# Edge tiles of a graph kernel: a 16-bit view of the source one-hots in place of a copy, and the fourth source one-hot made on ScalarE

## The chip, the cores and the metric

The kernel runs on one NeuronCore of a Trainium2 chip as a single launch. The metric is the device time of one execution in microseconds (us); lower is better. The engines are named as in the profile: PE (TensorE matmuls), PEld (TensorE weight loads), DVE (VectorE), ACT (ScalarE), POOL (GpSimd) and SP (the queue that issues most transfers). A "q" behind an engine's name marks its sequencer, which handles registers, waits and DMA issues.

## What is computed

Four graph layers follow one another on 3,125 nodes of 128 features and 103,125 edges. The stage of this case is the edge pass of the first layer, and what later layers need of the edges is gathered in the same pass:

```python
edge_index = jnp.stack([src, dst])
h = jnp.maximum(_layernorm(x), 0.0)
# layer 0: one message per edge, summed at the edge's source
msg_input = jnp.concatenate([h[dst], edge_feats], axis=1)
m = leaky_relu(msg_input @ msg_w1 + msg_b1)
messages = m @ msg_w2 + msg_b2
aggregated = segment_sum(messages, src, num_segments=3125)
# layers 1 to 3 sum over the same edges at dst: plain, or weighted by rel_table[etype]
```

## The kernel before, in words

An earlier stage sorts the edges by (source tile, destination tile). The edge stage then takes them in tiles of 128 edges, four tiles (`G` = 4) to a group. There are 1,504 tiles, so 376 groups, handled as 47 passes of `RING` = 8 groups (`LOOPS` = 47). The first pass and the last are written out; on VectorE the 45 passes between run as one hardware loop with a body of eight steps, in which semaphore counts come from registers.

For each group the stage builds one-hot matrices that place edges at nodes, and multiplies with them:

- `ohd` (16 bit): destination one-hots, four tiles in one VectorE instruction (function `onehots` on VectorE).
- `ohs` (32 bit): source one-hots. GpSimd makes the first three tiles (`onehots` on GpSimd, semaphore `s_os`), VectorE the fourth (`source_onehot`, semaphore `s_o3`).
- `ohs16`: a 16-bit copy of `ohs`, made by ScalarE in one instruction (line 1014). In the profile buffer numbers are dropped, so it is printed as `ohs_e` too.
- `ohw`: `ohd` scaled by each edge's relation weight, four ScalarE instructions (line 1016).
- TensorE turns `ohd` (`pdt`, line 1041), ScalarE copies that to `dT` (line 1007), and TensorE multiplies `dT` with node projections into `px`, three matmuls a tile (line 1070).
- VectorE adds the rows of the edges to `px`, which gives `pre` (function `add`, line 1125). ScalarE makes the negative part (`excess`, line 1000), GpSimd adds both to `hid` (line 973), and TensorE sums `hid` over the sources into `ps` (line 1081). VectorE adds `ps` to `S` (line 1151).
- The pair products `pm` are two matmuls a tile: `ohs16` by `ohd` (line 1063) and `ohs` by `ohw` (line 1064). `pm` has two halves, tiles 0 and 1 of a group in the one, tiles 2 and 3 in the other. VectorE adds each tile's `pm` to a running sum `acc` (function `collect`, line 1137), one after the other, since each sum starts from the one before.

No planner sets the order; each engine's `step` writes it by hand. A VectorE step is: collect tile 0, `source_onehot` of the next group, collect tile 1, `add`, a table lookup into a register (`place`, lines 62 and 1130), collect tile 2, `onehots`, collect tile 3, `sums`. In TensorE's `tiles`, the first matmul of tile 2 waits until the collects have freed the second half of `pm`, that is until tile 3 of the group before has been collected:

```python
if j % 2 == 0 and not (first and kp < 1):
    pe.wait_ge(s_acc, (m - 1) * G + 2 * q + 2)
```

The last `px` matmul of the step raises `s_x`, for which `add` waits.

Of the kernel before, what the change touches and what calls it, by code (L numbers as in the profile page):

```python
# [15 lines left out]
BF16 = mybir.dt.bfloat16  # L16
I32 = mybir.dt.int32
ALU = mybir.AluOpType
ACT = mybir.ActivationFunctionType
# [3 lines left out]
P = 128  # L23
D = 128
# [14 lines left out]
G = 4  # L39
RING = 8  # L40
BUFS = 4
# [13 lines left out]
def back(i, k, n):  # L55

    return (i + (k - n) // RING if (k - n) // RING else i), (k - n) % RING
# [21 lines left out]
def build(nc, x, src, dst, ea, et, w1, b1, w2, b2, u1, c1, u2, c2,  # L79
# [6 lines left out]
    with ExitStack() as top:  # L86
# [3 lines left out]
        def sem(name):  # L90
            return top.enter_context(nc.semaphore(name))
# [5 lines left out]
        iota128 = tsb("iota128", [P, P])  # L97
# [5 lines left out]
        ones = tsb("ones", [P, P])  # L103
# [31 lines left out]
        with ExitStack() as srt:  # L135
            def sb(name, shape, dt=F32):
                return srt.enter_context(nc.sbuf_tensor(name, shape, dt))
# [727 lines left out]
        with ExitStack() as ctx:  # L865
# [9 lines left out]
            ohd = sb("ohd_e", [P, BUFS, G, P], BF16)  # L875
            ohw = sb("ohw_e", [P, BUFS, G, P])
            ohs = sb("ohs_e", [P, BUFS, G, P])
            ohs16 = sb("ohs16_e", [P, BUFS, G, P], BF16)
            dT = sb("dT", [P, 2, G, P], BF16)
            pre = sb("pre_e", [P, 2, G, P])  # L880
            excess = sb("excess", [P, 2, G, P])
# [9 lines left out]
            s_od = sem("e_dst_onehots")  # L891
            s_os = sem("e_src_onehots")
            s_o3 = sem("e_last_src_onehot")
            s_o16 = sem("e_src_onehots16")
            s_td = sem("e_dst_turned")
            s_cd = sem("e_dst_copied")
            s_x = sem("e_hidden")
# [56 lines left out]
            @block.gpsimd  # L954
            def _(pool):
                def onehots(i, k, first):
                    n = i * RING + k
                    pool.wait_ge(s_rt[k // 2], i * 16 + 16)
                    if not (first and k < BUFS):
                        pool.wait_ge(s_sp, n - BUFS + 1)  # L960
                        pool.wait_ge(s_o16, n - BUFS + 1)
                    pool.sem_inc(s_go, 1)
                    for j in range(G - 1):
                        last = nc.gpsimd.tensor_scalar(ohs[:, k % BUFS, j, :], iota128[:], rt[:, k, j, D + 1:D + 2], None, ALU.is_equal)  # L964
                    last.then_inc(s_os, 1)

                def leaky(i, k, first):
                    n = i * RING + k
                    pool.wait_ge(s_y, n + 1)
                    if not (first and k < 2):  # L970
                        pool.wait_ge(s_sp, n - 1)
                    pool.sem_inc(s_go, 1)
                    nc.gpsimd.tensor_tensor(hid[:, k % 2, :, 0:D], pre[:, k % 2, :, :], excess[:, k % 2, :, :],  # L973
                                            ALU.add).then_inc(s_g, 1)

                onehots(0, 0, True)
                for k in range(RING):
                    onehots(*back(0, k, -1), k + 1 < RING)
                    if k:
                        leaky(0, k - 1, True)  # L980
                    else:
                        nc.gpsimd.memset(S[:], 0.0).then_inc(s_sz, 1)
                with pool.Fori(1, LOOPS - 1) as i:
                    for k in range(RING):
                        onehots(*back(i, k, -1), False)
                        leaky(*back(i, k, 1), False)
                for k in range(RING):
                    if k + 1 < RING:
                        onehots(LOOPS - 1, k + 1, False)
                    leaky(*back(LOOPS - 1, k, 1), False)  # L990
                leaky(LOOPS - 1, RING - 1, False)

            @block.scalar
            def _(act):
                def negative(i, k, first):
                    n = i * RING + k
                    act.wait_ge(s_pre, n + 1)
                    if not (first and k < 2):
                        act.wait_ge(s_g, n - 1)
                    nc.scalar.activation(excess[:, k % 2, :, :], pre[:, k % 2, :, :], ACT.Relu, scale=-0.8).then_inc(s_y, 1)  # L1000

                def step(i, k, first, final):
                    n = i * RING + k
                    if not (first and k < 2):
                        act.wait_ge(s_x, n - 1)
                    act.wait_ge(s_td, n + 1)
                    nc.scalar.activation(dT[:, k % 2, :, :], pdt[:, k % 2, 0:G, :], ACT.Copy).then_inc(s_cd, 1)  # L1007
                    if not (first and k < 1):
                        negative(*back(i, k, 1), first)
                    if not (first and k < BUFS):  # L1010
                        act.wait_ge(s_m, 2 * (n - BUFS) + 2)
                    act.wait_ge(s_os, n + 1)
                    act.wait_ge(s_o3, n + 1)
                    nc.scalar.activation(ohs16[:, k % BUFS, :, :], ohs[:, k % BUFS, :, :], ACT.Copy).then_inc(s_o16, 1)  # L1014
                    for j in range(G):
                        last = nc.scalar.activation(ohw[:, k % BUFS, j, :], ohd[:, k % BUFS, j, :], ACT.Copy, scale=rt[:, k, j, D + 2:D + 3])  # L1016
                    last.then_inc(s_ow, 1)
                    if not (first and k == 0):
                        load_freed(act, i, k, final)

                for k in range(RING):
                    step(0, k, True, False)
                with act.Fori(1, LOOPS - 1) as i:
                    for k in range(RING):
                        step(i, k, False, False)
                for k in range(RING):
                    step(LOOPS - 1, k, False, True)
                negative(LOOPS - 1, RING - 1, False)

            @block.tensor  # L1030
            def _(pe):
# [12 lines left out]
                def tiles(hid_of, pair_of, first):  # L1044
# [9 lines left out]
                    if pair_of:  # L1054
                        ip, kp = pair_of
                        m = ip * RING + kp
                        pe.wait_ge(s_ow, m + 1)
                    for j in range(G):
                        if pair_of:
                            q = j // 2  # L1060
# [43 lines left out]
            def _(dve):  # L1104
# [45 lines left out]
                    Sv = S[:, ds(st, 1), :].squeeze(1)  # L1150
                    nc.vector.tensor_tensor(Sv, Sv, ps[:, k % 2, 0:D + 1], ALU.add).then_inc(s_sa, 1)

                def source_onehot(i, k, first):

                    n = i * RING + k
                    dve.wait_ge(s_rt[k // 2], i * 16 + 16)
                    if not (first and k < BUFS):
                        dve.wait_ge(s_sp, n - BUFS + 1)
                    nc.vector.tensor_scalar(ohs[:, k % BUFS, G - 1, :], iota128[:], rt[:, k, G - 1, D + 1:D + 2], None,
                                            ALU.is_equal).then_inc(s_o3, 1)  # L1160

                def step(i, k, first, final):

                    one, two, three = (not (first and k < n) for n in (1, 2, 3))
                    if two:
                        collect(*back(i, k, 2), first, 0)
                    if not (final and k == RING - 1):
                        source_onehot(*back(i, k, -1), first and k + 1 < RING)
                    if two:
                        collect(*back(i, k, 2), first, 1)  # L1170
                    if one:
# [13 lines left out]

                onehots(0, 0, True)
                onehots(0, 1, True)
                source_onehot(0, 0, True)
                for k in range(RING):
                    step(0, k, True, False)  # L1190
                with dve.Fori(1, LOOPS - 1) as i:
# [1026 lines left out]
```

## Time and profile before

| what | value |
|---|---|
| time of a run, median of 3 | 3433.16 us |
| lowest and highest of the 3 | 3431.87 and 3433.22 us |
| profiled execution, span from first to last instruction | 3432.5 us |
| first and last `collect` of the edge stage | 1330.4 and 2637.1 us from the span's start |
| granted TensorE clock through the edge stage | 1.00 of full speed |

The span is the profiled execution's own time; it lies 0.7 us under the median of the runs. Times in the rows further down count from the span's start. A row of a timeline gives start, duration, engine, line and operation, what is written and read, how many instructions are merged, and in brackets how long the engine had been idle and who ended that. Idle times of some tens of nanoseconds are not printed.

### The profile page before, as it was taken

What the parts mean: (1) busy time and instruction counts of PE and PEld (TensorE: products, weight loads), DVE (VectorE), ACT (ScalarE), POOL (GpSimd) and SP (SyncE); (2) the same over time, 40 slices, a digit from 0 to 9 for tenths busy, and PEclk for the clock granted to TensorE, in tenths of its full rate; (3) what the DMA queues carried; (4) which work ended last, traced back from release to release, by engine and by line L of the source; (5) the groups of instructions that cost most, each with busy time, mean ns of one, the idle gap of its engine ahead of it and who ended that gap; (6) DMA issues with size and microseconds to landing.
All of it is one profiled execution on the core that took longest, in us unless ns stands there. A gap on an engine that the chain in (4) does not pass through costs nothing. (4 is left out here: it accounts for less than half of the span.)

```text
span 3432.5 us, 87712 instructions
## 1 busy us (share of the span) xinstructions
PE 2529.2 (74%) x20390; PEld 1959.9 (57%) x20391; DVE 2686.0 (78%) x8325; ACT 1648.7 (48%) x4130; POOL 1979.1 (58%) x2344
## 2 busy tenths in 40 slices
PE   2433555555555555999999999999999329989899
PEld 1322334443334434888888888888887214444454
DVE  8853777777777765999999999999997779993501
ACT  2011222222222224888888888888886655452200
POOL 1005777777777777888888888888887000000000
PEclk9976666677666677999999999999999559999999
DMA  9993222222222215888888888888887569868766
GB/s 382 412 414 117 79 78 78 78 78 83 78 77 78 78 63 145 230 227 229 230 227 228 231 225 228 231 227 230 228 227 244 215 284 352 300 235 304 250 218 203
DMA packets 738172, 696.85 MB, mean 203 GB/s; under 512 B 48523, under 2 KB 637274, under 8 KB 734778
## 3 DMA queue, kind: packets, MB, share of 16 engines
q1 hardware_dynamic: 516770, 536.77, 46.7%
q10 hardware_dynamic: 195544, 104.71, 12.6%
q0 software_dynamic: 25792, 54.52, 4.8%
q8 instruction: 37, 0.61, 0.1%
q14 instruction: 29, 0.24, 0.0%
HBM read 340.91 MB, written 354.90 MB: 203 GB/s over the span
## 5 line engine op out<-in xcount | busy, mean ns | idle before, releaser
L855 POOL DMA_INDIRECT sorted_rows<-rows,posi x806 | 784.1, 973 | 338.9 <-issue 316.6
L1137 DVE SCALAR_TENSOR_TENSOR acc<-acc,keep,pm 128x256 f32<-128x256 f32 x1504 | 717.4, 477 | 23.0 <-issue 8.3
L964 POOL TENSOR_SCALAR ohs_e<-iota,rt 128x128 f32<-128x128 f32 x1128 | 663.6, 603 | 12.5 <-DMA rt<-sorted_rows 12.5
L1064 PE MATMUL pm<-ohw_e,ohs_e 128*128 128x128 f32 x3008 | 662.6, 302 | 0.0
L803 PE MATMUL s_peq<-sb_w1bb,eT 128*128 128x256 f32 x806 | 352.2, 531 | 397.7 <-ACT eT L658 378.8
L973 POOL TENSOR_TENSOR hid<-pre_e,excess 128x512 f32<-128x512 f32 x376 | 511.8, 1361 | 141.6 <-ACT excess L1000 141.6
L1070 PE MATMUL px<-PN,dT 128*128 x4512 | 498.3, 219 | 0.1
L1016 ACT ACTIVATE ohw_e<-ohd_e,rt 128x128 f32<-128x128 bf16 x1504 | 474.6, 386 | 0.0
L1064 PEld LDWEIGHTS pm<-ohw_e,ohs_e 128*128 128x128 f32 x3008 | 459.4, 193 | 0.0
L803 PEld LDWEIGHTS s_peq<-sb_w1bb,eT 128*128 128x128 f32 x806 | 172.6, 264 | 439.4 <-ACT eT L658 431.1
L1081 PE MATMUL ps<-hid,ohs_e 128*128 128x129 f32 x3008 | 417.9, 281 | 1.2 <-POOL hid L973 1.1
L1070 PEld LDWEIGHTS px<-PN,dT 128*128 128x128 bf16 x4512 | 382.4, 99 | 18.2 <-issue 0.3
L1063 PE MATMUL pm<-ohd_e,ohs_e 128*128 128x128 bf16 x1504 | 334.0, 222 | 48.2 <-DVE acc L1137 11.8
L1081 PEld LDWEIGHTS ps<-hid,ohs_e 128*128 128x128 f32 x3008 | 365.5, 191 | 1.7 <-POOL hid L973 1.5
L1000 ACT ACTIVATE excess<-pre_e 128x512 f32<-128x512 f32 x376 | 237.3, 631 | 255.2 <-DVE pre_e L1125 255.2
L721 DVE SCALAR_TENSOR_TENSOR junkR<-s_binrows,binc,later 128x128 bf16<-128x128 f32 x806 | 235.1, 346 | 77.8 <-PE s_binrows L776 77.8
L651 ACT ACTIVATE rows<-lo 128x26 f32 (+1 forms) x62 | 15.4, 249 | 543.9 <-DMA sorted_rows<-rows,posi 468.7
L1125 DVE TENSOR_TENSOR pre_e<-px,rt 128x512 f32<-128x512 f32 x376 | 258.6, 688 | 14.6 <-PE px L1070 3.4
L1117 DVE TENSOR_TENSOR ohd_e<-iota,rt 128x512 bf16<-128x512 bf16 x376 | 257.1, 684 | 0.2 <-DVEq L1109 0.2
L1007 ACT ACTIVATE dT<-pdt 128x512 bf16<-128x512 bf16 x376 | 216.0, 575 | 40.3 <-PE pdt L1041 40.3
L1014 ACT ACTIVATE ohs_e<-ohs_e 128x512 bf16<-128x512 f32 x376 | 230.5, 613 | 0.0
L701 DVE SCALAR_TENSOR_TENSOR junkW<-iotar,typc,relt 128x100 bf16<-128x100 f32 x806 | 224.7, 321 | 2.2
(317 smaller groups left out, 4275.0 us busy)
## 6 DMA issues: line engine op xcount, KB each, us to landing
count_matrices<-acc SPq DMA_DIRECT2D x1504, 128.0 KB, 2.4
sorted_rows<-zrow SPq DMA_DIRECT2D x188, 528.0 KB, 10.1
rt<-sorted_rows ACTq DMA_DIRECT2D x184, 528.0 KB, 4.5
gab<-count_matrices SPq DMA_DIRECT2D x60, 1280.0 KB, 6.0
arb<-count_matrices SPq DMA_DIRECT2D x25, 1664.0 KB, 9.0
ab<-count_matrices SPq DMA_DIRECT2D x25, 1600.0 KB, 9.0
arb<-count_matrices SPq DMA_DIRECT2D x25, 1536.0 KB, 8.4
ef<-in_edge_attr_dram SPq DMA_DIRECT2D x58, 364.0 KB
```

What stands on the lines that cost most here:

```text
L803: nc.tensor.matmul(pe_q[:, q % 2, 0:2 * D], eT[:, q % 2, :], w1bb[:], start=True, stop=True).then_inc(s_q, 1)
L855: pool.indirect_dma_start(sortd, bass.IndirectOffsetOnAxis(ap=posi[:, h, c:c + 1], axis=0), rows[:, h, c, :], None).then_inc(s_sc[h], 16)
L964: last = nc.gpsimd.tensor_scalar(ohs[:, k % BUFS, j, :], iota128[:], rt[:, k, j, D + 1:D + 2], None, ALU.is_equal)
L973: nc.gpsimd.tensor_tensor(hid[:, k % 2, :, 0:D], pre[:, k % 2, :, :], excess[:, k % 2, :, :], ALU.add).then_inc(s_g, 1)
L1016: last = nc.scalar.activation(ohw[:, k % BUFS, j, :], ohd[:, k % BUFS, j, :], ACT.Copy, scale=rt[:, k, j, D + 2:D + 3])
L1063: nc.tensor.matmul(pm[:, q, j % 2, 0:P], ohs16[:, kp % BUFS, j, :], ohd[:, kp % BUFS, j, :], start=True, stop=True)
L1064: last = nc.tensor.matmul(pm[:, q, j % 2, P:2 * P], ohs[:, kp % BUFS, j, :], ohw[:, kp % BUFS, j, :], start=True, stop=True)
L1070: last = nc.tensor.matmul(px[:, kh % 2, j, :], dT[:, kh % 2, j, :], PN[:, ds(dt[j], 1), part, :].squeeze(1), start=(part == 0), stop=(part ...
L1081: last = nc.tensor.matmul(ps[:, k % 2, 0:D + 1], ohs[:, k % BUFS, j, :], hid[:, k % 2, j, :], start=(j == 0), stop=(j == G - 1))
L1117: nc.vector.tensor_tensor(ohd[:, k % BUFS, :, :], iota16[:].unsqueeze(1).to_broadcast([P, G, P]), rt[:, k, :, D:D + 1].to_broadcast([P, G, ...
L1125: nc.vector.tensor_tensor(pre[:, k % 2, :, :], px[:, k % 2, :, :], rt[:, k, :, 0:D], ALU.add).then_inc(s_pre, 1)
L1137: nc.vector.scalar_tensor_tensor(acc[:, k % SUMS, j, :], before, keep[:, at:at + 1] if isinstance(at, int) else keep[:, ds(at, 1)], pm[:, ...
```

## The change

The 16-bit copy `ohs16` goes: the name becomes a view of `ohs` that takes the upper 16 bits of each 32-bit value, so the matmul at line 1063 loads its weights with a step of two 16-bit elements. The upper half of the 32-bit numbers 0 and 1 are the 16-bit numbers 0 and 1. The fourth source one-hot moves from VectorE to ScalarE as two instructions: `distances` takes the absolute value of (column minus source) into a new tile `far`, and `nearest` takes Relu(1 - `far`). TensorE now waits for the source one-hots itself, and GpSimd no longer waits for the copy.

```diff
-            ohs16 = sb("ohs16_e", [P, BUFS, G, P], BF16)
+            ohs16 = ohs[:].bitcast(BF16).rearrange("p b j (c h) -> p b j c h", h=2)[:, :, :, :, 1]
+            far = sb("far_e", [P, 2, P])
...
-            s_o16 = sem("e_src_onehots16")
+            s_far = sem("e_last_src_distances")
...
-                        pool.wait_ge(s_o16, n - BUFS + 1)
...
+                def distances(i, k, first):
+                    n = i * RING + k
+                    act.wait_ge(s_rt[k // 2], i * 16 + 16)
+                    if not (first and k < 2):
+                        act.wait_ge(s_o3, n - 1)
+                    nc.scalar.activation(far[:, k % 2, :], iota128[:], ACT.Abs, bias=rt[:, k, G - 1, D + 1:D + 2],
+                                         scale=-1.0).then_inc(s_far, 1)
+
+                def nearest(i, k, first):
+                    n = i * RING + k
+                    act.wait_ge(s_far, n + 1)
+                    if not (first and k < BUFS):
+                        act.wait_ge(s_sp, n - BUFS + 1)
+                    nc.scalar.activation(ohs[:, k % BUFS, G - 1, :], far[:, k % 2, :], ACT.Relu, bias=ones[:, 0:1],
+                                         scale=-1.0).then_inc(s_o3, 1)
...
+                    distances(i, k, first)
...
-                    act.wait_ge(s_os, n + 1)
-                    act.wait_ge(s_o3, n + 1)
-                    nc.scalar.activation(ohs16[:, k % BUFS, :, :], ohs[:, k % BUFS, :, :], ACT.Copy).then_inc(s_o16, 1)
...
+                    nearest(i, k, first)
...
+                        pe.wait_ge(s_os, m + 1)
+                        pe.wait_ge(s_o3, m + 1)
...
-                def source_onehot(i, k, first):
...
-                    if not (final and k == RING - 1):
-                        source_onehot(*back(i, k, -1), first and k + 1 < RING)
```

In the built program, an `ISA` or `REGISTER_ALU` row is a sequencer instruction on registers; a wait in brackets stands on that row and holds up what follows. On VectorE, in the second step of the loop's body, these rows stood from the collect of tile 0 to `pre`:

```order
L1137 SCALAR_TENSOR_TENSOR acc<-acc,keep,pm 128x256
L1158 REGISTER_ALU [waits e_rows1]
L1159 TENSOR_SCALAR ohs_e<-iota,rt 128x128 [waits e_group_sums]
L1134 REGISTER_ALU
L1137 ISA [waits e_accumulated]
L1137 SCALAR_TENSOR_TENSOR acc<-acc,keep,pm 128x256
L1122 REGISTER_ALU
L1125 TENSOR_TENSOR pre_e<-px,rt 128x512 [waits e_leaky,e_hidden]
```

In the changed kernel the same place reads:

```order
L1154 SCALAR_TENSOR_TENSOR acc<-acc,keep,pm 128x256
L1151 REGISTER_ALU
L1154 ISA [waits e_accumulated]
L1154 SCALAR_TENSOR_TENSOR acc<-acc,keep,pm 128x256
L1139 REGISTER_ALU
L1141 REGISTER_ALU [waits e_hidden]
L1142 TENSOR_TENSOR pre_e<-px,rt 128x512 [waits e_leaky]
```

The one-hot is gone, the collect of tile 1 still waits for that of tile 0 (`e_accumulated`) on the register row ahead of it, and the wait for `px` (`e_hidden`) has moved from `pre` itself to a register row ahead of `pre`. In the body's other seven steps it stays on `pre`.

On TensorE, at the start of the loop's body, these rows lead to the first pair product before:

```order
L62 TENSOR_LOAD tilei
L1051 REGISTER_ALU
L1053 REGISTER_ALU [waits e_dst_copied]
L1062 ISA [waits e_weighted_onehots,e_pre]
L1063 MATMUL pm<-ohd_e,ohs_e 128x128 [waits e_accumulated]
```

And in the changed kernel:

```order
L62 TENSOR_LOAD tilei
L1066 REGISTER_ALU
L1068 REGISTER_ALU [waits e_dst_copied]
L1079 ISA [waits e_src_onehots,e_last_src_onehot,e_weighted_onehots,e_pre]
L1080 MATMUL pm<-ohd_e,ohs_e 128x128 [waits e_accumulated]
```

Two waits are added there, as in every step; the matmuls and their order stay.

On ScalarE, the rows of a step of the body from the copy or the weighted one-hots to `dT` were:

```order
L1014 ACTIVATE ohs_e<-ohs_e 128x512 [waits e_last_src_onehot,e_src_onehots,e_pair_products]
L1016 ACTIVATE ohw_e<-ohd_e,rt 128x128 x4
L1006 REGISTER_ALU [waits e_hidden]
L1007 ACTIVATE dT<-pdt 128x512 [waits e_dst_turned]
L1000 ACTIVATE excess<-pre_e 128x512 [waits e_leaky,e_pre]
```

They are now:

```order
L1030 ACTIVATE ohw_e<-ohd_e,rt 128x128 [waits e_pair_products]
L1030 ACTIVATE ohw_e<-ohd_e,rt 128x128 x3
L1014 REGISTER_ALU [waits e_last_src_distances]
L1015 ACTIVATE ohs_e<-far_e,ones 128x128 [waits e_group_sums]
L1007 ACTIVATE far_e<-iota,rt 128x128 [waits e_last_src_onehot,e_rows1]
L1023 REGISTER_ALU [waits e_hidden]
L1024 ACTIVATE dT<-pdt 128x512 [waits e_dst_turned]
```

One instruction of 512 columns ahead of the weighted one-hots is replaced by two of 128 columns behind them. No table load stands among the body's ScalarE rows in either kernel.

## Rows read from the trace of the kernel before

**Rows 1.** The page's first line.

```profile
span 3432.5 us, 87712 instructions
```

**Rows 2.** Stretches: busy us and instructions per engine, PE clock, DMA share, GB/s.

```profile
2000.00:2100.00 100.00, 96.40 (x1039) 89.89 (x1040) 97.66 (x231) 80.50 (x202) 89.32 (x116) 1.00 0.84 229
```

**Rows 3.** Timeline of VectorE, one step of the loop (start, duration in us).

```profile
2000.12 0.48 DVE L1137 SCALAR_TENSOR_TENSOR acc<-acc,keep,pm 128x256 f32<-128x256 f32 x1
2000.52 0.29 DVE L1159 TENSOR_SCALAR ohs_e<-iota,rt 128x128 f32<-128x128 f32 x1
2000.74 0.48 DVE L1137 SCALAR_TENSOR_TENSOR acc<-acc,keep,pm 128x256 f32<-128x256 f32 x1
2001.26 0.69 DVE L1125 TENSOR_TENSOR pre_e<-px,rt 128x512 f32<-128x512 f32 x1
2001.98 0.48 DVE L1137 SCALAR_TENSOR_TENSOR acc<-acc,keep,pm 128x256 f32<-128x256 f32 x1
...
2002.98 0.47 DVE L1137 SCALAR_TENSOR_TENSOR acc<-acc,keep,pm 128x256 f32<-128x256 f32 x1
...
2004.72 0.69 DVE L1125 TENSOR_TENSOR pre_e<-px,rt 128x512 f32<-128x512 f32 x1
```

**Rows 4.** Timeline of TensorE's matmuls, same stretch.

```profile
2000.89 0.33 PE L1070 MATMUL px<-PN,dT 128*128 x3
...
2003.51 0.23 PE L1063 MATMUL pm<-ohd_e,ohs_e 128*128 128x128 bf16 x1
...
2004.36 0.33 PE L1070 MATMUL px<-PN,dT 128*128 x3
2004.52 1.11 PE L1081 MATMUL ps<-hid,ohs_e 128*128 128x129 f32 x8
2005.47 0.39 PE L1041 MATMUL pdt<-ident,ohd_e 128*128 128x128 bf16 x4
```

**Rows 5.** Waits from 1600 to 2500 us: total us, times, longest us.

```profile
ACT excess L1000 <- DVE pre_e L1125: 175.7, 259, 1.0
...
PEld pm L1063 <- DVE acc L1137: 76.9, 255, 0.4
```

**Rows 6.** Sequencer instructions of two lines: count, ns min/median/max, first and last start.

```profile
L62 DVEq TENSOR_LOAD <-tilei x259: 303/308/440, 1601.3 to 2498.6; - x130
...
L1057 PEldq EVENT_SEMAPHORE  x259: 51/51/51, 1602.2 to 2498.9; - x130
```

**Rows 7.** Timeline of VectorE, first two steps of a loop pass.

```profile
2021.18 0.48 DVE L1137 SCALAR_TENSOR_TENSOR acc<-acc,keep,pm 128x256 f32<-128x256 f32 x1 [0.20 <-issue]
...
2021.87 0.47 DVE L1137 SCALAR_TENSOR_TENSOR acc<-acc,keep,pm 128x256 f32<-128x256 f32 x1
2022.26 0.68 DVE L1125 TENSOR_TENSOR pre_e<-px,rt 128x512 f32<-128x512 f32 x1
2022.86 0.46 DVE L1137 SCALAR_TENSOR_TENSOR acc<-acc,keep,pm 128x256 f32<-128x256 f32 x1
...
2025.61 0.68 DVE L1125 TENSOR_TENSOR pre_e<-px,rt 128x512 f32<-128x512 f32 x1
2026.31 0.48 DVE L1137 SCALAR_TENSOR_TENSOR acc<-acc,keep,pm 128x256 f32<-128x256 f32 x1
```

**Rows 8.** Timeline of TensorE's matmuls, same two steps.

```profile
2019.83 0.23 PE L1063 MATMUL pm<-ohd_e,ohs_e 128*128 128x128 bf16 x1
...
2020.84 0.23 PE L1063 MATMUL pm<-ohd_e,ohs_e 128*128 128x128 bf16 x1
...
2021.69 0.33 PE L1070 MATMUL px<-PN,dT 128*128 x3
...
2025.22 0.33 PE L1070 MATMUL px<-PN,dT 128*128 x3
```

**Rows 9.** Timeline of ScalarE: the copy and the four weighted one-hots.

```profile
2002.52 0.61 ACT L1014 ACTIVATE ohs_e<-ohs_e 128x512 bf16<-128x512 f32 x1
...
2003.04 1.26 ACT L1016 ACTIVATE ohw_e<-ohd_e,rt 128x128 f32<-128x128 bf16 x4
```

More of the change, by code:

```diff
@@ L1151, in sums @@
                     nc.vector.tensor_tensor(Sv, Sv, ps[:, k % 2, 0:D + 1], ALU.add).then_inc(s_sa, 1)
-                def source_onehot(i, k, first):
[L1155 to L1160, printed above, removed]
                 def step(i, k, first, final):
@@ L1187, in _ @@
                 onehots(0, 1, True)
-                source_onehot(0, 0, True)
                 for k in range(RING):
```

## The prediction

> **What bounds the kernel now.** I read the stretches first. Every 100 us of the edge stage look like [rows 2]: VectorE busy 97.7, TensorE 96.4, GpSimd 89, ScalarE 80.5, all at full TensorE clock. That invites the reading "VectorE is the bound, so taking an instruction from it pays". Two engines at 96 and 98% do not say which one the other waits for, so I went to the timelines of one step, looking for gaps between an end and the next start.
>
> The step takes 3.46 us (`pre` at 2001.26 and at 2004.72, [rows 3]). Follow it from the collect of tile 3. That ends at 2002.98 + 0.47 = 2003.45, and TensorE starts tile 2's pair product at 2003.51 [rows 3, 4]. It had been idle: the waits say that weight loads of `pm` waited for `acc` in 255 of 259 steps, 76.9 us in all, 0.30 us each [rows 5]. TensorE then does the second half of its tiles, whose last `px` ends at 2004.36 + 0.33 = 2004.69, and VectorE starts `pre` at 2004.72, 0.03 later [rows 3, 4]. One step earlier it is the same: `px` ends at 2001.22, `pre` starts at 2001.26. Yet the collect before it started at 2000.74, and two VectorE instructions that do not wait for each other start some 0.40 apart here (collect of tile 0 to the one-hot, 2000.12 to 2000.52); `pre` could have gone at 2001.14. So `pre` waits for TensorE, only too briefly to be printed. From `pre` it is 0.72 to the collect of tile 2 and 1.00 from there to that of tile 3, which closes the ring:
>
> 0.47 + 0.06 + 1.18 + 0.03 + 0.72 + 1.00 = 3.46 us.
>
> That is the whole step. The 0.72 is more than the 0.60 that `pre` needs before the next instruction may start (2022.26 to 2022.86, [rows 7], where VectorE was late). The difference is the sequencer: held at `pre` by the wait, it only then begins the table lookup, 0.31 us for the load alone [rows 6], and the register work for the next collect.
>
> The removed one-hot is not in this ring. It stands between the collects of tiles 0 and 1, and these depend on each other: the first ends at 2000.60, the second starts at 2000.74, 0.13 to 0.14 later, with the one-hot done in between [rows 3]. The wait between them stands on a register row, and 0.13 is what that costs: 0.04 as at `pre`, where the wait is on the instruction itself, and some 0.09 for the register row.
>
> **The change part by part.**
>
> - *One-hot off VectorE.* 0.29 busy, 0.22 of start to start (2000.52 to 2000.74). In an ordinary step it filled a gap that the collects need anyway, and `pre` waits for TensorE behind it: worth 0. The gap stays, now empty.
> - *Copy off ScalarE, two short instructions on.* The copy held ScalarE for 0.52 (2002.52 to 3.04); the one-hots on 128 columns take 1.26 for four, so at most 0.32 each [rows 9]. I take the new two at that price, since they have the same width and one operand per partition like them: 0.64 − 0.52 = +0.12 a step. ScalarE idles 175.7 / 259 = 0.68 us a step waiting for `pre` [rows 5], so 0. Below, nothing excludes their being as short as nothing; above, the 0.61 of the copy each would be +0.70, just more than the cover, but that row has four times the columns. Queued behind them are the load of rows several steps ahead and `dT`; `dT` moves by the same +0.12, which would lie under the 0.30 for which TensorE waits later in its step. GpSimd's dropped wait was not one that ended last: 0.
> - *Weights with a step of two.* No row shows such a load. Nearest are the contiguous 16-bit ones, with `px` matmuls 0.16 / 3 = 0.05 apart (2004.36 to 2004.52), and the 32-bit ones of `ps`, whose columns also lie 4 bytes apart, at (2005.47 − 2004.52) / 8 = 0.12 [rows 4]. So a load costs between 0 and +0.065 more. Tiles 0 and 1 are covered by the 0.30 of waiting; tiles 2 and 3 are in the ring, so 0 to 0.13 a step, 0 to 49 us over 376 steps. I take 0, the nearer row by width of the numbers loaded: the 16-bit matmuls stand an even 0.05 apart, so no load sticks out there, and a longer one has that 0.05 to hide behind.
> - *Two more waits on TensorE.* Both signals are a step old when asked for, so only the sequencer's time counts. An event wait lasts 0.05 [rows 6]; with the step to the next instruction I take 0.09, as for the register row, with bounds 0.05 and 0.13. In ordinary steps the 0.30 covers it. In the body's first step it does not: there tile 0 starts at 2019.83, late, and tile 2 follows 1.01 behind at 2020.84 with no wait printed [rows 8].
> - *Moved wait in the second step.* Instead of on `pre`, the wait for `px` stands on a register row ahead of it: +0.09, bounds 0 and 0.13.
>
> At the loop's turn these must be worked out together [rows 7, 8]. First step, before: `px` ends at 2022.02, but VectorE, slow through the branch, starts `pre` only at 2022.26 and the next collect at 2022.86. After: TensorE 0.09 later, so `px` ends at 2022.11 and the wait lets `pre` go at 2022.15. VectorE has the collect of tile 0 done at 2021.66, that of tile 1 starts at 2021.79 (it was 2021.87) and `pre` at 2022.18. The sequencer needs 0.72 from 2022.15: collect of tile 2 at 2022.87, +0.01. The one place where the one-hot was in the way gives back its gain to the added waits. Second step, before: `px` ends at 2025.55, `pre` at 2025.61, collect at 2026.31. After: 2025.56 + 0.04 + 0.09 = 2025.69, and 0.72 more is 2026.41, +0.10. So +0.10 a pass, 45 passes: **+4.5 us**.
>
> Bounds of the same sum. With both waits free, the first step's collect comes at 2022.78 (−0.08) and the second keeps that: −3.6 us. With 0.13 for each: first +0.05, second +0.18, +8.1 us. The passes written out at either end hold constants in place of registers and no moved wait: 0.
>
> Sum: 3432.5 [rows 1] + 4.5 = 3437.0 us of span, and with the 0.7 by which the median lies above it, 3437.7 us. A measurement of this kernel tells a change from none at about 0.2%, 6.9 us, so this is "no change that can be told", on the slow side.
>
> **The rivals.**
>
> - *Strided weights are slow.* Place: the two 16-bit loads behind the wait for `acc`. It decides as soon as such a load outlasts the 0.05 of the matmul it hides behind; at the pace of the `ps` rows it gives 3437.7 + 49 = about 3487 us. For it: the ring has no slack there. Against: 16-bit loads are not what limits the 0.05, as far as the even spacing shows. The Trainium skill (TensorE: Matmul & The Clock Gate, section "Weight-path perf modes — Fast Weight Load (FWL) and DoubleRow") has a rule that speaks against the change: a fast load reads 32 bits at a time, two 16-bit values; it also allows column steps other than one. By that rule every read here would bring one useful value, a load twice as long; no run so far shows whether that still fits under the matmul. Chance 0.13.
> - *VectorE is the bound after all.* If the 0.22 came back in each of 376 steps: −83 us, 3351 us; if only the 0.12 by which `pre` comes behind its engine's earliest start, −45 us, 3388 us. For it: 97.7% busy. Against: `pre` starts 0.03 to 0.04 behind `px` in both steps shown, and the second collect 0.13 behind the first. Chance 0.06.
> - *ScalarE becomes late.* It needs its step to grow by 0.68, against +0.12 and perhaps 0.13 for each of three register waits. At 0.1 beyond, 38 us slower, 3471 us. Chance 0.04.
> - *The turn costs nothing.* The added waits hide, and the first step's 0.08 is kept: 3430 us. It lies in the bounds above and in the same verdict.
>
> **How the numbers follow.** The ring unchanged, with a turn between −3.6 and +8.1: chance 0.77, that is 3429.6 to 3441.3 us, most of it within 6.9 us of before; I put 0.60 there, 0.15 above and 0.02 below. Slower by over 0.2%: 0.15 + 0.13 + 0.04 = 0.32. Faster: 0.06 + 0.02 = 0.08. Within: 0.60. The strided loads could cost a small part of their bound (a tenth is 5 us, a quarter 12), so the range reaches to 3437.7 + 12 = 3450 above and to 3428 below; that leaves out about 2 in 10.
>
> **What would show it.** Right: an ordinary step still 3.46 us, with the collect of tile 1 still 0.13 behind that of tile 0 and `pre` 0.04 behind `px`; VectorE's busy share down by 0.2 / 3.46, some 6%, with no time won; `pre` about 0.13 behind `px` in the second step of a pass. Wrong: matmuls of tiles 2 and 3 spread out by more than 1.18 (weights), ScalarE's wait for `pre` gone, or an ordinary step shorter than 3.4 us.

## The result, and the profile after

The changed kernel takes 3442.01 us (median of 20 runs) against 3435.76 us of the kernel before in the same comparison (20 runs): ratio 1.0016, 95% interval 1.0009 to 1.0022. One run of the kernel before, at 4389.77 us, lies far outside all others and is left out of the ratio; the quotient of the two medians is 1.0018. The kernel is slower by less than the 0.2% that the prediction set as its bound (the interval reaches a little beyond it), on the side and in the case that it called likeliest; predicted were 3437.7 us with a range of 3428 to 3450. Of the 4.3 us between forecast and measurement, 2.6 are the kernel before itself: the forecast started from its earlier median of 3433.16. The change was put at +4.5 us and measured +6.25.

The page's first line, the stretch that answers to [rows 2] (busy us and instructions per engine, TensorE clock, DMA share, GB/s), the waits that answer to [rows 5] (total us, times, longest us), and the collects of the whole edge stage (count, ns min/median/max, first and last start) in the profile after:

```profile
span 3444.6 us, 87849 instructions
```

```profile
2000.00:2100.00 100.00, 95.65 (x1033) 89.01 (x1031) 92.95 (x202) 82.55 (x232) 88.54 (x115) 1.00 0.83 225
```

```profile
ACT excess L1000 <- DVE pre_e L1142: 163.4, 258, 1.0
...
PEld pm L1080 <- DVE acc L1154: 83.1, 257, 0.5
```

```profile
L1154 DVE SCALAR_TENSOR_TENSOR acc<-acc,keep,pm x1504: 468/480/483, 1331.7 to 2645.3; 128x256 f32<-128x256 f32 x188
```

VectorE is busy 4.7 of 100 us less than before, and the kernel is not faster: the time went into VectorE's waiting. The prediction had named some 6 of 100. But of the one-hot's 0.29 us only the 0.14 between the two collects (2000.60 to 2000.74 in [rows 3]) were not covered by the collects themselves, which is 4 of 100; the longer pass gives most of the rest. TensorE waits for `acc` a little longer (0.32 us each, it was 0.30), and ScalarE still waits 163.4 / 258 = 0.63 us a step for `pre` (it was 0.68). From its first to its last collect the edge stage takes 2645.3 − 1331.7 = 1313.6 us. The same row of the kernel before:

```profile
L1137 DVE SCALAR_TENSOR_TENSOR acc<-acc,keep,pm x1504: 461/479/483, 1330.4 to 2637.1; 128x256 f32<-128x256 f32 x188
```

There it is 1306.7, so the stage is 6.9 us longer. That agrees with the 6.25 us between the medians. The two profiled spans differ by 12.1; of the other 5 us, 1.3 lie ahead of the stage's first collect and 3.9 behind its last, where the loop plays no part, and single executions of one kernel here differ by as much.

An ordinary step, VectorE first (answers to [rows 3]; "x2" are two instructions in one row, the second 1.09 − 0.48 = 0.61 behind the first), then TensorE (answers to [rows 4]):

```profile
2003.88 0.48 DVE L1154 SCALAR_TENSOR_TENSOR acc<-acc,keep,pm 128x256 f32<-128x256 f32 x1
...
2004.48 1.09 DVE L1154 SCALAR_TENSOR_TENSOR acc<-acc,keep,pm 128x256 f32<-128x256 f32 x2
2005.62 0.69 DVE L1142 TENSOR_TENSOR pre_e<-px,rt 128x512 f32<-128x512 f32 x1
2006.34 0.48 DVE L1154 SCALAR_TENSOR_TENSOR acc<-acc,keep,pm 128x256 f32<-128x256 f32 x1
...
2007.34 0.47 DVE L1154 SCALAR_TENSOR_TENSOR acc<-acc,keep,pm 128x256 f32<-128x256 f32 x1
...
2009.09 0.69 DVE L1142 TENSOR_TENSOR pre_e<-px,rt 128x512 f32<-128x512 f32 x1
```

```profile
2004.41 0.23 PE L1080 MATMUL pm<-ohd_e,ohs_e 128*128 128x128 bf16 x1 [0.22 <-DVE acc L1154]
...
2005.25 0.33 PE L1087 MATMUL px<-PN,dT 128*128 x3
...
2007.88 0.23 PE L1080 MATMUL pm<-ohd_e,ohs_e 128*128 128x128 bf16 x1
```

The ring is the old one, link by link. Collect of tile 3 ends at 2004.36, tile 2 starts at 2004.41, `px` ends at 2005.58, `pre` starts at 2005.62, the next collects come 0.72 and 1.00 later, and from `pre` to `pre` it is 3.47 us. The collects of tiles 0 and 1 are 0.61 apart, as they were with the one-hot between them (0.62 in [rows 3]).

The loss is in the first two steps of a loop pass. VectorE, then TensorE (these answer to [rows 7, 8]):

```profile
2025.67 1.10 DVE L1154 SCALAR_TENSOR_TENSOR acc<-acc,keep,pm 128x256 f32<-128x256 f32 x2 [0.32 <-PE pm L1081]
2026.69 0.68 DVE L1142 TENSOR_TENSOR pre_e<-px,rt 128x512 f32<-128x512 f32 x1
2027.30 0.48 DVE L1154 SCALAR_TENSOR_TENSOR acc<-acc,keep,pm 128x256 f32<-128x256 f32 x1
...
2030.12 0.69 DVE L1142 TENSOR_TENSOR pre_e<-px,rt 128x512 f32<-128x512 f32 x1
2030.86 0.48 DVE L1154 SCALAR_TENSOR_TENSOR acc<-acc,keep,pm 128x256 f32<-128x256 f32 x1
```

```profile
2022.59 0.33 PE L1087 MATMUL px<-PN,dT 128*128 x3
...
2024.32 0.23 PE L1080 MATMUL pm<-ohd_e,ohs_e 128*128 128x128 bf16 x1 [0.23 <-POOL ohs_e L964]
...
2029.67 0.33 PE L1087 MATMUL px<-PN,dT 128*128 x3
```

Second step: `px` ends at 2030.00 and `pre` starts 0.12 behind it (0.06 in [rows 7, 8]), then 0.74 to the collect. First step: TensorE begins tile 0 1.73 after it began the last `px` of the step before (2022.59 to 2024.32), and the collect of tile 0 follows 1.35 behind that start. Before, that last `px` was this row:

```profile
2018.22 0.33 PE L1070 MATMUL px<-PN,dT 128*128 x3
```

Tile 0 began at 2019.83 [rows 8]. That is 1.61, and from there to the collect of tile 0 at 2021.18 [rows 7] it was 1.35 as well. So in both kernels the first collect of a pass waits for TensorE, although the row of before put its idle time down to "issue"; and TensorE is 0.12 later. The row of tile 0 after puts its idle time down to GpSimd's one-hots (`<-POOL ohs_e`). They were no longer being waited for: those of this group had ended at 2017.23, and ScalarE's fourth at 2022.31. What is new there is the time that the added waits take in TensorE's sequencer.

Below, the length of a step is the time between the ends of its last collect and of the one before, as the median over 44 of the loop's 45 passes (from the middle of the first to the middle of the last); a "pass" is the sum of the eight steps' means. Before: 3.536, 3.466 and six times 3.466, a pass of 27.82 us. After: 3.600, 3.567 and six times 3.467, a pass of 27.98. So +0.064 and +0.101 us; a pass is 0.163 longer, and 45 × 0.163 = 7.3 us.

### The profile page after: what moved, and what is told of

Read it like the earlier page. It is cut to its first block and busy times, and to the rows that moved or that the text cites. A ratio compares the mean times of both kernels' runs of the same rounds, so it can differ in the third digit from the quotient of the medians.

```text
span 3444.6 us, 87849 instructions
## 1 busy us (share of the span) xinstructions
PE 2532.9 (74%) x20390; PEld 1961.0 (57%) x20391; DVE 2632.6 (76%) x7949; ACT 1673.2 (49%) x4506; POOL 1977.4 (57%) x2344
## 5 line engine op out<-in xcount | busy, mean ns | idle before, releaser
L642 ACT ACTIVATE rows<-s_peq 128x256 f32<-128x256 f32 x403 | 153.9, 382 | 130.8 <-PE s_peq L803 129.0
```

## The experiments

The theory: a ring through TensorE's second half, `pre` and the collects of tiles 2 and 3 sets the step; the removed one-hot is outside it, and the loss comes from where three waits stand. The main rivals: VectorE's sum of work is the bound; the strided weights cost something. Ratios are to the kernel before.

**The view alone.** The kernel before, with the 16-bit view in place of the copy; VectorE keeps its one-hot and ScalarE the waits.

```diff
-ohs16 = sb("ohs16_e", [P, BUFS, G, P], BF16)
+ohs16 = ohs[:].bitcast(BF16).rearrange("p b j (c h) -> p b j c h", h=2)[:, :, :, :, 1]
...
-nc.scalar.activation(ohs16[:, k % BUFS, :, :], ohs[:, k % BUFS, :, :], ACT.Copy).then_inc(s_o16, 1)
```

> Only the 16-bit view in place of the copy; ScalarE keeps its waits for the source one-hots, so TensorE needs none, and VectorE keeps the fourth one-hot. My theory (the step is the ring through the collect of tile 3, TensorE's second half, pre and the collect of tile 2; the change costs only the two added waits in the first step of a pass and the moved wait in the second): nothing of that is in here, so a pass of 8 steps takes 27.82 us as before, TensorE's second half 1.18 us, ratio 0.9995 to 1.0005. Rival, the strided weights cost something: second half over 1.18 us, ratio above 1.001.

3433.42 us, ratio 1.0003 (0.9994 to 1.0012). A pass is 27.82 us, and TensorE's second half, from its first weight load to the end of its last `px`, lasts 1.179 us, where it was 1.178. The rows of the loads themselves (from 1600 to 2500 us: count, busy us, mean ns), of the kernel before and of this run:

```profile
L1063 PEld LDWEIGHTS pm<-ohd_e,ohs_e 128*128 128x128 bf16 x1036 | 100.7, 97 | 78.7 <-DVE acc L1137 76.9 <-issue 1.1
```

```profile
L1060 PEld LDWEIGHTS pm<-ohd_e,ohs_e 128*128 128x128 bf16 x1036 | 101.0, 98 | 78.4 <-DVE acc L1134 77.5 <-issue 0.3
```

97 and 98 ns: no longer load is to be seen. The strided weights are free and the copy's removal brings nothing.

**The two added waits alone**, on the kernel before:

```diff
 pe.wait_ge(s_ow, m + 1)
+pe.wait_ge(s_os, m + 1)
+pe.wait_ge(s_o3, m + 1)
```

> The kernel before with only the two waits added on TensorE (copy and fourth one-hot stay). My theory: they cost 0.12 us in the first step of each of the 45 passes, since the collect of tile 0 there waits for TensorE, and nothing in the other seven: a pass takes 27.94 us, +5.6 us in all, ratio about 1.0016. Rival, waits for signals that are long there are free: 27.82 us, ratio 1.000.

3432.27 us, ratio 0.9998 (0.9989 to 1.0007). A pass is 27.88 us: only the first step changes, 3.536 to 3.592. Its place was right and its size half of what was expected. TensorE's tile 0 comes 0.11 later and the collect of tile 0 with it, but the collect of tile 1 then follows 0.614 behind, where it was 0.687, so 0.07 of the delay is taken up in the gap where the one-hot stands. 45 × 0.055 = 2.5 us is less than the ratio can show.

**No fourth one-hot.** The kernel before, without VectorE's one-hot after the first pass (so the sums use old one-hots for the fourth tile) and without the waits for it.

```diff
-if not (final and k == RING - 1):
+if first and k + 1 < RING:
     source_onehot(*back(i, k, -1), first and k + 1 < RING)
```

> The kernel before, but VectorE makes the fourth source one-hot only in the first pass and leaves it out after (the old contents are used, so sums over that tile are of other edges); copy and all else stay. My theory: the one-hot fills a gap between two collects that depend on each other, so ordinary steps stay at 3.467 us; the first step of a pass gains some 0.07, the second loses it again to the wait that moves to a register row: a pass within 0.05 of 27.82 us, ratio 0.999 to 1.001. Rival, VectorE's own time sets the step: 0.12 to 0.22 us less a step, 45 to 83 us, ratio 0.976 to 0.987.

3435.64 us, ratio 1.0009 (0.9999 to 1.0018). VectorE has one instruction less in every step, nobody does its work, and nothing is gained: six steps stay at 3.466, the first is 3.500 (−0.04), the second 3.567 (+0.10). The moved wait thus comes from the one-hot's absence in VectorE's program, not from anything on TensorE or ScalarE.

**The waits on ScalarE.** The changed kernel without TensorE's two waits; ScalarE asks for GpSimd's one-hots, and its own last one-hot gives the signal that TensorE waited for anyway.

```diff
-pe.wait_ge(s_os, m + 1)
-pe.wait_ge(s_o3, m + 1)
...
+act.wait_ge(s_os, n + 1)
 for j in range(G):
-    last = nc.scalar.activation(ohw[...], ohd[...], ACT.Copy, scale=...)
-last.then_inc(s_ow, 1)
+    nc.scalar.activation(ohw[...], ohd[...], ACT.Copy, scale=...)
...
-scale=-1.0).then_inc(s_o3, 1)
+scale=-1.0).then_inc(s_ow, 1)
```

> The changed kernel, with the two added waits taken off TensorE: ScalarE waits for GpSimd's three one-hots before it scales the target one-hots, and its own last one-hot now counts for the signal that TensorE waited for anyway. Theory: the first step of a pass loses its 0.06 us to these two waits alone, and without them it shows the gain of the missing VectorE one-hot, 3.50 us as in the run without the fourth one-hot (3.600 in the changed kernel, 3.536 before); the second step keeps its +0.10 (3.567); a pass is about 27.89 us against 27.985 in the changed kernel and 27.82 before, the edge stage about 1309.7 us, ratio to the kernel before about 1.0009. Rival (the first step is lost to ScalarE's extra instructions or to the tile addresses, not to TensorE's waits): the first step stays near 3.60, a pass at 27.98, ratio 1.0016 to 1.002. Ordinary steps 3.466 under both.

3434.92 us, ratio 1.0007 (0.9998 to 1.0016). First step 3.504, second 3.568, a pass 27.90, as the theory said. TensorE's tile 0 is back where it was, so the first step's loss is that of these two waits.

**The waits swapped.** The run before, with the two waits of VectorE's `add` in the other order, so that the one that ends last stands on the instruction:

```diff
-dve.wait_ge(s_x, n + 1)
 if not (first and k < 2):
     dve.wait_ge(s_g, n - 1)
+dve.wait_ge(s_x, n + 1)
```

> The run before, and in VectorE's add the two waits in the other order, the one on GpSimd's sums first, so that the wait that ends last stands on the instruction itself in every step, as it does in the kernel before. Theory: the second step's +0.10 is the price of where this wait stands; the lag from the last px matmul to pre falls from 0.127 to about 0.04 there, the step from 3.567 to 3.466, and with the first step at 3.50 a pass is about 27.79 us, 0.03 under the kernel before: stage about 1306 us, ratio 0.9995. Rival (the second step is late because of what the branch leaves in the sequencer, whichever wait stands where): the second step stays at 3.567, a pass at 27.89, ratio 1.0009.

3432.43 us, ratio 0.9998 (0.9989 to 1.0007). In its trace, TensorE's last `px` of a second step and VectorE's `pre` behind it, with the collect:

```profile
2024.99 0.33 PE L1083 MATMUL px<-PN,dT 128*128 x3
```

```profile
2025.36 0.69 DVE L1138 TENSOR_TENSOR pre_e<-px,rt 128x512 f32<-128x512 f32 x1
2026.07 0.48 DVE L1150 SCALAR_TENSOR_TENSOR acc<-acc,keep,pm 128x256 f32<-128x256 f32 x1
```

`pre` starts 0.04 behind the end of `px` at 2025.32, not 0.12, and the second step is 3.467. A pass is 27.79, 0.03 under the kernel before: all that the removed one-hot is worth where it is. Both losses are undone.

**The lookup early.** The changed kernel, with VectorE's table lookup taken from behind `pre` to between the collects of tiles 0 and 1:

```diff
     collect(*back(i, k, 2), first, 0)
+if three:
+    st = place(*back(i, k, 3))
 if two:
     collect(*back(i, k, 2), first, 1)
 if one:
     add(*back(i, k, 1), first)
...
-if three:
-    st = place(*back(i, k, 3))
```

> The changed kernel with the table lookup moved from behind pre into the gap between the collects of tiles 0 and 1 that the one-hot left. My theory: the sequencer's work behind pre shrinks, pre to the next collect falls from 0.725 to 0.60 us in seven of eight steps, an ordinary step to 3.345 us: 45 x 7 x 0.12 = 38 us less than the changed kernel, 31 us less than before, ratio about 0.991. Rival, VectorE's busy time or TensorE's is the bound: no change against the changed kernel, ratio 1.002.

3407.22 us, ratio 0.9924 (0.9910 to 0.9937). VectorE in an ordinary step:

```profile
2000.24 0.48 DVE L1154 SCALAR_TENSOR_TENSOR acc<-acc,keep,pm 128x256 f32<-128x256 f32 x1 [0.23 <-DVE acc L1154]
2000.64 0.69 DVE L1142 TENSOR_TENSOR pre_e<-px,rt 128x512 f32<-128x512 f32 x1
2001.24 0.47 DVE L1154 SCALAR_TENSOR_TENSOR acc<-acc,keep,pm 128x256 f32<-128x256 f32 x1
...
2003.97 0.69 DVE L1142 TENSOR_TENSOR pre_e<-px,rt 128x512 f32<-128x512 f32 x1
```

From `pre` to the collect it is 0.60 to 0.61 in place of 0.72, and the step falls with it, 3.466 to 3.342. No engine does less work than in the changed kernel. This shows the ring, and that the sequencer's work behind `pre` is in it. The first step is longer, 3.798 for 3.600: the collects of tiles 0 and 1, which are on the path there, stand 0.07 further apart with the lookup between them; the other 0.13 is explained below, with the run that keeps the lookup late in that step.

**The lookup early, in the kernel before**, where the one-hot still stands in that gap:

```diff
     source_onehot(*back(i, k, -1), first and k + 1 < RING)
+if three:
+    st = place(*back(i, k, 3))
...
-if three:
-    st = place(*back(i, k, 3))
```

> The kernel before, with VectorE's table lookup moved to between the collects of tiles 0 and 1, behind the one-hot that still stands there. Theory (the ring): what the sequencer does behind pre is on the path, so the ordinary step falls from 3.466 to about 3.34 here too, as in the changed kernel with the same move (3.342), unless one-hot and lookup together make the collect of tile 1 so late that pre is late: collect of tile 1 to pre takes 0.52, and the gap of 0.61 may grow to 0.9 before VectorE and not TensorE ends last. So 3.34 to 3.45 a step, ratio 0.991 to 0.999; where it lies in this range says how much of the room for the lookup the removed one-hot makes. Rival (VectorE's instructions are the bound and the room is made by the change alone): 3.46 or more a step, ratio 1.000 or above.

3435.39 us, ratio 1.0005 (0.9996 to 1.0014). VectorE in the fourth step of a pass:

```profile
2007.45 0.32 DVE L1159 TENSOR_SCALAR ohs_e<-iota,rt 128x128 f32<-128x128 f32 x1
2008.07 0.48 DVE L1137 SCALAR_TENSOR_TENSOR acc<-acc,keep,pm 128x256 f32<-128x256 f32 x1 [0.30 <-issue]
2008.47 0.69 DVE L1125 TENSOR_TENSOR pre_e<-px,rt 128x512 f32<-128x512 f32 x1
```

Six steps are 3.35 to 3.43, in the range given; but the first is 4.00 and the fourth 3.61, and a pass is 27.91, no better than before. With one-hot and lookup in one gap the collects of tiles 0 and 1 are 0.76 apart and more (1.02 in the step above, whose first collect starts at 2007.05), and `pre` follows the collect of tile 1 without a pause: VectorE has become the bound. So the removed one-hot does make room, worth 27.91 − 27.29 = 0.62 us a pass, some 28 us in all, but only once something from the ring is put there. Why the fourth step is 0.2 longer than its neighbours isn't settled.

**All three together**, on the changed kernel: the waits on ScalarE, the swapped waits and the early lookup.

> The changed kernel with the waits placed as in the run with the swapped waits, and the table lookup between the collects of tiles 0 and 1. Theory: ordinary steps 3.342 as in the run with the lookup alone, the second step's +0.09 gone (3.43 to 3.34), the first step 3.80 less the 0.10 that TensorE's two waits cost it, 3.70: a pass 27.1 us against 27.29 there, the edge stage 1275 us, ratio to the kernel before 0.990. Rival (the first step's extra 0.30 under the early lookup has swallowed these two losses): a pass 27.29, ratio 0.9924.

3399.87 us, ratio 0.9902 (0.9887 to 0.9918); a pass is 27.08, its first step 3.667. The gains add.

**The same, with the lookup late in the first step:**

```diff
-if three:
+if three and k:
     st = place(*back(i, k, 3))
...
+if three and not k:
+    st = place(*back(i, k, 3))
```

> The run before, but in the first step of a pass the lookup stays behind pre, where it was. Theory: in the first step VectorE comes late from the branch and every microsecond of its sequencer lies on the path, so there the early lookup costs 0.2 to 0.3 instead of gaining 0.12; with it late the first step is 3.50 as in the run with the swapped waits and the other seven 3.34: a pass 26.9 us, the edge stage 1266 us, ratio 0.988. Rival (the step after the turn takes the delay over, as the ring must be filled again): a pass 27.05 to 27.1, ratio 0.990.

3398.62 us, ratio 0.9894 (0.9879 to 0.9910), a pass of 27.03. The seven steps came out, the first did not: 3.608, where 3.50 was expected. The rival's number was near and its reason wrong, for the second step is 3.341. TensorE around the turn of the loop:

```profile
2027.11 0.33 PE L1083 MATMUL px<-PN,dT 128*128 x3
2028.72 0.23 PE L1076 MATMUL pm<-ohd_e,ohs_e 128*128 128x128 bf16 x1
```

Again 1.61 from the last `px` to tile 0, as before the change. At the turn the path leaves VectorE's collects of tiles 2 and 3 and runs through TensorE from `px` on, so the 0.12 that the lookup gives back behind `pre` is not in it; it only makes the measured step start earlier. This and the run before, which can't be told apart, are the fastest versions that leave no work out.

**The target one-hots in the gap too.** This starts from all three together and moves VectorE's target one-hots into the same gap, with eight buffers for them:

```diff
     collect(*back(i, k, 2), first, 0)
+if not (final and k >= RING - 2):
+    onehots(*back(i, k, -2), first and k + 2 < RING)
...
 if two:
     collect(*back(i, k, 2), first, 2)
-if not (final and k >= RING - 2):
-    onehots(*back(i, k, -2), first and k + 2 < RING)
```

> The changed kernel with the waits placed as in the two runs above, the lookup between the collects of tiles 0 and 1, and the target one-hots moved to there too, from between the collects of tiles 2 and 3 (with eight buffers in place of their ring, so that they wait for nothing late). Theory: collect of tile 2 to collect of tile 3 is 1.00 us of the ring only because these one-hots stand between; without them it is about 0.61, so VectorE's part of the ring shrinks by 0.39, of which TensorE's own work allows only some: its matmuls take about 3.2 us a step. The step falls from 3.342 to 3.20 to 3.25, a pass to 26.0 to 26.4 us, the edge stage to 1225 to 1240 us, ratio to the kernel before 0.976 to 0.980. Rival (VectorE's total of instructions is the bound: moving them changes nothing): step 3.34, ratio 0.991. A third way: the gap overflows, the collect of tile 1 comes late enough for pre to wait for VectorE, and the step ends at 3.3 to 3.45.

3526.06 us, ratio 1.0265 (1.0251 to 1.0279): none of the three numbers. The collects of tiles 2 and 3 did come 0.60 apart, but most steps take 3.68. VectorE's one-hots, and GpSimd in the same microseconds:

```profile
2005.08 1.16 DVE L1130 TENSOR_TENSOR ohd_e<-iota,rt 128x512 bf16<-128x512 bf16 x1
```

```profile
2004.42 1.28 POOL L971 TENSOR_TENSOR hid<-pre_e,excess 128x512 f32<-128x512 f32 x1 [0.24 <-ACT excess L998]
2005.67 2.20 POOL L962 TENSOR_SCALAR ohs_e<-iota,rt 128x128 f32<-128x128 f32 x3
```

They last 1.16 in place of 0.69, and end 0.54 after GpSimd's addition ends (2006.24 against 2005.70).

**The target one-hots behind the collect of tile 3**, the group sums in their place. The "run before" of this expectation is the one with the lookup late in the first step:

```diff
-if not (final and k >= RING - 2):
-    onehots(*back(i, k, -2), first and k + 2 < RING)
+if three:
+    sums(*back(i, k, 3), first, st)
 if two:
     collect(*back(i, k, 2), first, 3)
-if three:
-    sums(*back(i, k, 3), first, st)
+if not (final and k >= RING - 2):
+    onehots(*back(i, k, -2), first and k + 2 < RING)
```

> The run before, and VectorE's target one-hots behind the collect of tile 3, with the short addition of group sums in their old place between the collects of tiles 2 and 3. Theory (the ring): collect of tile 2 to that of tile 3 falls from 1.00 to 0.61, which TensorE's matmuls, about 3.2 us a step, cannot follow whole; VectorE's own row of starts is 0.60 (pre) + 0.61 + 0.39 + 0.61 (one-hots) + 0.65 + 0.39 = 3.25, so 3.22 to 3.27 a step, a pass 26.0 to 26.4, ratio 0.976 to 0.981. Rival (as where they stood between the collects of tiles 0 and 1: the one-hots run beside GpSimd's work and last 1.15 in place of 0.69, and then VectorE is the bound): 3.5 to 3.7 a step, ratio 1.00 to 1.03. Which of the two, the duration of one such instruction tells.

3588.28 us, ratio 1.0448 (1.0434 to 1.0462), a pass of 31.22. VectorE's one-hots and GpSimd again:

```profile
2004.26 1.77 DVE L1130 TENSOR_TENSOR ohd_e<-iota,rt 128x512 bf16<-128x512 bf16 x1
```

```profile
2004.21 1.27 POOL L971 TENSOR_TENSOR hid<-pre_e,excess 128x512 f32<-128x512 f32 x1 [0.85 <-ACT excess L998]
```

The rival was right, and worse than it said: 1.77, ending at 2006.03, once more 0.55 after GpSimd's addition (2005.48). In half of the steps it is so, and the step behind it takes 4.3. In the other half VectorE's instruction begins first, and GpSimd's addition is the longer one:

```profile
2019.92 0.68 DVE L1130 TENSOR_TENSOR ohd_e<-iota,rt 128x512 bf16<-128x512 bf16 x1
```

```profile
2019.95 1.78 POOL L971 TENSOR_TENSOR hid<-pre_e,excess 128x512 f32<-128x512 f32 x1 [0.33 <-ACT excess L998]
```

Behind these the step takes 3.21 (the second and the fourth of a pass) or about 3.8 (the third and the fifth).

**GpSimd nearly idle.** The run before, leaving out nearly all of GpSimd's work after the first pass: one column of 128, and one tile of three in its one-hots, so sums and hidden values are not those of the reference.

```diff
-nc.gpsimd.tensor_tensor(hid[:, k % 2, :, 0:D], pre[:, k % 2, :, :], excess[:, k % 2, :, :],
+nc.gpsimd.tensor_tensor(hid[:, k % 2, :, 0:w], pre[:, k % 2, :, 0:w], excess[:, k % 2, :, 0:w],
...
```

> The run with the target one-hots behind the collect of tile 3, with nearly all of GpSimd's work left out after the first pass: one column in place of 128 in its one-hots (one tile in place of three) and in its addition, so the sums are of other edges and the hidden values are not formed. Theory: the 1.77 us that VectorE's target one-hots take there are a collision with GpSimd's instructions, so with GpSimd idle they take 0.69 in every step, and the steps fall from 3.8 on the mean to the 3.21 that the run shows in the steps without a collision: a pass 25.7 to 26.2 us, ratio to the kernel before about 0.972 to 0.980. Rival (they are slow there because of something else that runs at that place, TensorE's or ScalarE's reads or the transfers): 1.77 us stays, steps of 3.8 to 4.3, ratio above 1.03.

3348.76 us, ratio 0.9746 (0.9718 to 0.9774), a pass of 25.97 with steps of 3.225. VectorE's target one-hots from 1600 to 2500 us (count, busy us, mean ns), in this run and in the one before it:

```profile
L1132 DVE TENSOR_TENSOR ohd_e<-iota,rt 128x512 bf16<-128x512 bf16 x277 | 192.8, 696 | 0.0
```

```profile
L1130 DVE TENSOR_TENSOR ohd_e<-iota,rt 128x512 bf16<-128x512 bf16 x232 | 284.5, 1226 | 0.0
```

0.70 for 1.23 on the mean: it is GpSimd's work that makes them slow.

## Why the prediction was right, and the step of it that was off

- *The ring and the one-hot worth nothing in an ordinary step.* Shown three ways. The step stays at 3.466 with the one-hot gone (changed kernel, and the run without a fourth one-hot), and it falls by 0.12 when the lookup, which the prediction had put into the ring, leaves it, though no busy time is saved. The rival "VectorE is the bound" is out for this order of instructions, and 97.7% busy was no evidence for it.
- *ScalarE.* The two new instructions were put at 0.12 more than the copy. ScalarE's wait for `pre` fell by 0.05 a step, its busy share rose by 2 of 100: less than put, and hidden either way.
- *Strided weights at 0.* Shown by the view alone, 1.179 against 1.178 us for the second half. The Trainium skill's rule that a fast weight load reads 32 bits at a time (TensorE: Matmul & The Clock Gate, section "Weight-path perf modes — Fast Weight Load (FWL) and DoubleRow") would, as an estimate from it, make such a load twice as long; here nothing of that reaches the step, and the load's own rows in the run with the view alone are no longer either (98 against 97 ns).
- *The second step, +0.09 by itself* (the +0.10 a pass counts the first step's 0.01 as well). It measured +0.10, for the reason given: `pre` comes 0.127 behind `px`, where the prediction had 0.13 (0.04 and 0.09 for the register row). It vanishes when the two waits change places.
- *The first step, +0.01.* This term was mis-sized: it measured +0.06. The prediction had VectorE "slow through the branch" and kept the collect of tile 0 fixed, done at 2021.66, so that TensorE's added waits could act only through `px`. In fact that collect waits for TensorE itself: it starts 0.35 behind the last pair product of tile 1 in both kernels and in every run but the two whose target one-hots were slow (0.38 and 2.11), and 1.35 behind tile 0's start in both kernels. So the waits' 0.11 (put at 0.09) delay the whole chain of collects, and the 0.07 that the missing one-hot brings between the collects of tiles 0 and 1 is taken off: 0.05, with `pre` to the collect of tile 2 unchanged at 0.60; 0.005 more in each of two other pauses make the 0.06. The runs with the waits alone (+0.055), without the one-hot alone (−0.036) and with the waits on ScalarE (back to 3.504) bear out both parts. The two don't simply add, since the 0.07 in the gap can be won only once.
- *The sum.* 45 × 0.163 = 7.3 us for +4.5, inside its own bound of +8.1. The verdict did not hang on the term that was off: the +4.5 put, the +6.25 between the medians and the +7.3 of the passes are 0.13 to 0.21% of the kernel.

## What to carry to other kernels

Before pricing a removed instruction, close the ring: list end-to-start links until their sum is the period, and ask whether the instruction is a link. A freed gap is worth what can be moved into it from a link; here the sequencer's table lookup, worth 0.9% against the changed kernel, and it did not fit before the change made room. Before moving work into a gap, look at what the other engines do in it. And the steps at a loop's turn have a path of their own: follow each first instruction there back to its signal, even where the row says "issue".

## What the runs showed of the hardware

- VectorE's target one-hots (two SBUF operands, 0.68 us) and GpSimd's addition (two SBUF operands, 1.27 us) held each other up here: where the two overlapped, the one that began first kept its length and the other ended late. With the addition first, VectorE's instruction ended 0.54 and 0.55 behind it in the rows above, whether it had begun 0.66 or 0.05 after it. With VectorE first, the addition took 1.78. With GpSimd nearly idle, VectorE kept to 0.70. The Trainium skill says this (SBUF — State Buffer, section "Who interferes with whom"): an operation of VectorE with two inputs in SBUF contends with a GpSimd instruction that reads SBUF, the shared ports are an exclusive lock, and the order of issue decides which of the two is held up. The trace agrees. In its old place VectorE's instruction begins 0.53 us ahead of the addition (2006.74 against 2007.27 in the changed kernel), so there VectorE loses nothing, and GpSimd little: its addition takes 1.29.
- A wait on a register row cost more than one on the instruction behind it: 0.127 against 0.037 from `px` to `pre`.
- Two more event waits, whose signals had long come, cost TensorE 0.11 us at the turn of the loop. In the other steps of the run with these waits alone they cost nothing (3.466 to 3.468): there TensorE comes to wait for `acc` later on.
